# V projection in tiles of one token block by eight heads, placed behind each step's scores

## The reference

```python
x = x + 0.5 * ffn(layernorm(x))          # 256 -> 1024, gelu, -> 256
x = x + attention(layernorm(x))          # 16 heads of 64, causal, ALiBi slopes, out projection 1024 -> 256
x = x + 0.5 * ffn(layernorm(x))          # the same ffn weights
```

## Time and profile before

| | us |
|---|---|
| median of 3 runs (lowest to highest) | 2167.85 (2166.65 to 2169.6) |
| the profiled execution | 2166.86 |
| its span, first to last instruction | 2165.1 |
| mean granted TensorE clock, share of full | 0.995 |
| busy in the span: TensorE, VectorE, ScalarE, GpSimd | 2127.4, 1498.8, 1238.3, 1054.7 |

### The profile page before, as it was taken

One profiled execution on the slowest core, in us unless ns is written; L12 is line 12 of the kernel. 1 busy time (PEld: TensorE's weight loads), 2 busy tenths in 40 slices (PEclk: granted clock), 3 DMA queues, 4 the chain that ended last, 5 costly groups with the idle time before them and its releaser, 6 DMA issues.

```text
span 2165.1 us, 41849 instructions
## 1 busy us (share of the span) xinstructions
PE 2127.4 (98%) x14720; PEld 1738.5 (80%) x14720; DVE 1498.8 (69%) x4029; ACT 1238.3 (57%) x3111; POOL 1054.7 (49%) x1770
## 2 busy tenths in 40 slices
PE   7999999999999999999999999999999999999997
PEld 5688787877878788787887878878787787878876
DVE  6766767667676676776768676676766767667664
ACT  4755746466464664736557365574646646466472
POOL 1744727446273553726537174462744627355371
PEclk9999999999999999999999999999999999999999
DMA  3422505234061341514315052250523405143151
GB/s 132 130 76 71 143 3 157 59 88 128 9 159 50 108 107 35 153 29 121 95 50 142 24 141 75 72 141 3 157 59 93 123 13 155 50 111 105 35 141 41
DMA packets 109985, 193.91 MB, mean 90 GB/s; under 512 B 34512, under 2 KB 53200, under 8 KB 109776
## 3 DMA queue, kind: packets, MB, share of 16 engines
q1 hardware_dynamic: 88816, 137.95, 22.7%
q0 software_dynamic: 20480, 52.47, 9.8%
q10 hardware_dynamic: 480, 0.82, 0.1%
HBM read 14.95 MB, written 8.39 MB: 11 GB/s over the span
## 4 chain that ended last, share of the span: by engine, by line
PE 92%; DVE 3%; ACT 1%; POOL 1%; SPq 1%; DMA 1%; issue 1%; POOLq 0%; DVEq 0%; ACTq 0%
PE ps L304 90%; PE ps L358 2%; DVE P L842 1%; SPq L247 1%; POOL P L1005 1%; ACT P L641 1%; POOL PT L247 0%; DMA PT<-P 0%; DVE gl L752 0%; DVE P L834 0%; DMA raw<-in_L_ffn_w 0%; DVE gh L801 0%; DVE st L761 0%; ACT gt L610 0%; DMA out_y<-x 0%
## 5 line engine op out<-in xcount | busy, mean ns | idle before, releaser
L1005 POOL TENSOR_SCALAR P<-P,rs 128x512 f32<-128x512 f32 (+3 forms) x1024 | 539.4, 546 | 419.9 <-DVE rs L825 416.5
L641 ACT ACTIVATE P<-P,mx 128x512 f32<-128x512 f32 (+3 forms) x1024 | 562.7, 552 | 183.9 <-DVE mx L834 183.6
L247 POOL DMA_DIRECT2D PT<-P x640 | 321.8, 508 | 250.4 <-DVE P L842 231.8
L842 DVE STREAM_TRANSPOSE P<-P 128x1792 f32<-128x1792 f32 (+1 forms) x256 | 372.3, 1483 | 7.2 <-POOL P L1005 6.6
L304 PE MATMUL ps<-PT,v 128*64 128x256 f32 (+1 forms) x3072 | 308.4, 350 | 11.3 <-DMA PT<-P 11.2
L304 PE MATMUL ps<-qk 64*128 64x512 f32 (+3 forms) x2048 | 311.0, 443 | 0.7 <-ACT qk L592 0.7
L304 PE MATMUL ps<-w2h,gh 128*128 128x256 f32 x1024 | 292.8, 286 | 0.5 <-DVE gl L752 0.5
L304 PEld LDWEIGHTS ps<-PT,v 128*64 128x64 f32 x3072 | 206.4, 138 | 107.9 <-issue 18.7
L304 PE MATMUL ps<-w2l,gh 128*128 128x256 f32 x1024 | 289.7, 283 | 0.0
L304 PE MATMUL ps<-w2h,gl 128*128 128x256 f32 x1024 | 289.6, 283 | 0.0
L592 ACT ACTIVATE qk<-ps 128x512 f32<-128x512 f32 x256 | 153.0, 598 | 230.6 <-PE ps L304 230.4
(11 more groups left out here) (85 smaller groups left out, 4387.7 us busy)
## 6 DMA issues: line engine op xcount, KB each, us to landing
PT<-P SPq DMA_DIRECT2D x1398, 80.0 KB, 2.6
PT<-P POOLq DMA_DIRECT2D x640, 80.0 KB, 2.7
x<-in_L_attn_x SPq DMA_DIRECT2D x16, 512.0 KB, 4.7
out_y<-x SPq DMA_DIRECT2D x15, 512.0 KB, 3.2
raw<-in_L_ffn_w SPq DMA_DIRECT2D x2, 512.0 KB, 5.9
raw<-in_L_ffn_w SPq DMA_DIRECT2D x1, 1024.0 KB, 8.8
rawq<-in_L_attn_w_qkv SPq DMA_DIRECT2D x1, 1024.0 KB, 7.2
rawk<-in_L_attn_w_qkv SPq DMA_DIRECT2D x1, 1024.0 KB, 9.3
```

Of the source, the lines that this page charges most:

```text
L247: e.dma_start(PT[c % 2][32 * m:32 * m + 32, g, :], P[c % 3][32 * g:32 * g + 32, m, :]).then_inc(landed.sem, 16)
L641: e.activation(p, p, ACT.Exp, bias=mx[:, r, i:i + 1], scale=-1.0, accum_out=sm[:, r, i:i + 1]).then_inc(s_ex.sem, 1)
L842: e.transpose(p, p).then_inc(s_tr.sem, 1)
L1005: e.tensor_scalar(p, p, rs[:, 2 * (c % 2) + h, i:i + 1], 1.0, ALU.mult, ALU.mult).then_inc(s_nz.sem, 1)
```

## The change

A V tile becomes one token block by eight heads: six matmuls with 512 columns moving, still one PSUM bank. There are still eight tiles: three stand at the front, and one in each of the steps 2 to 6. In a step the V tile now comes straight behind the scores, ahead of k and q; ScalarE copies it ahead of k, and copies q behind exps 2. The two V buffers hold eight heads each (8 KB per partition instead of 4 KB), so one serves the pairs 0 to 3 and the other 4 to 7. The 8 KB for that come from the space reserved for the descriptors of GpSimd's DMAs, which is cut to 8192 bytes; the kernel's own buffers begin at 8320 instead of 16512.

```diff
-    at = [16512]
+    at = [8320]
...
-    v = [place(f"v{i}", [128, NT, 4, DH], F32, V + 4096 * i) for i in range(2)]
+    v = [place(f"v{i}", [128, NT, 8, DH], F32, V + 8192 * i) for i in range(2)]
...
     def v_tiles(c):
-        return {6: [("v", 3, 0), ("v", 3, 1)], 7: []}.get(c, [("v", c // 2, c % 2)] if c >= 2 else [])
+        return {2: [("v", 0, 3)], 3: [("v", 1, 0)], 4: [("v", 1, 1)], 5: [("v", 1, 2)], 6: [("v", 1, 3)]}.get(c, [])
 
-    tiles = [("k", 0), ("q", 0), ("v", 0, 0), ("v", 0, 1)]
-    FIRST = 4
+    tiles = [("k", 0), ("q", 0), ("v", 0, 0), ("v", 0, 1), ("v", 0, 2)]
+    FIRST = 5
...
                 if tile[0] == "v":
-                    _, g, u = tile
-                    gs = slice(2 * HD + g * 256, 2 * HD + g * 256 + 256)
-                    for j in range(2):
-                        ts = slice((2 * u + j) * 128, (2 * u + j) * 128 + 128)
-                        last = three(dst[:, j * 256:j * 256 + 256],
-                                     [(xth[:, k, ts], xtl[:, k, ts], wqh[:, k, gs], wql[:, k, gs])
-                                      for k in range(NK)])
+                    _, g, t = tile
+                    gs = slice(2 * HD + g * 512, 2 * HD + g * 512 + 512)
+                    ts = slice(t * 128, t * 128 + 128)
+                    last = three(dst, [(xth[:, k, ts], xtl[:, k, ts], wqh[:, k, gs], wql[:, k, gs])
+                                       for k in range(NK)])
...
-                e.wait_ge(s_pc.sem, s_pc.at((b, ("v", c // 2, 1))))
+                e.wait_ge(s_pc.sem, s_pc.at((b, ("v", c // 4, 3))))
...
                 for c in range(2, NC):
                     scores(b, c)
+                    for tile in steps_v(b, c):
+                        proj_tile(b, tile)
                     if c + 1 < NC:
                         proj_tile(b, ("k", c + 1))
                         proj_tile(b, ("q", c + 1))
-                    for tile in steps_v(b, c):
-                        proj_tile(b, tile)
...
                     exps(b, c, 3)
+                    for tile in steps_v(b, c):
+                        proj_copy(b, tile)
                     if c + 1 < NC:
                         proj_copy(b, ("k", c + 1))
+                    exps(b, c, 2)
+                    if c + 1 < NC:
                         proj_copy(b, ("q", c + 1))
-                    exps(b, c, 2)
-                    for tile in steps_v(b, c)[:1]:
-                        proj_copy(b, tile)
                     exps(b, c, 0)
-                    for tile in steps_v(b, c)[1:]:
-                        proj_copy(b, tile)
                     exps(b, c, 1)
...
-    nc = bacc.Bacc("TRN2", target_bir_lowering=False, num_devices=1)
+    nc = bacc.Bacc("TRN2", target_bir_lowering=False, num_devices=1, dynamic_dma_scratch_size=8192)
```

More of the change, by code:

```diff
@@ L63, in build @@
     R = at[0]
-    QK, V, PP, PT_AT, GT = R, R + 8192, R + 16384, R + 47104, R + 67584
+    QK, V, PP, PT_AT, GT = R, R + 8192, R + 24576, R + 55296, R + 75776
     qk = [place(f"qk{i}", [128, 2, T], F32, QK + 4096 * i) for i in range(2)]
-    v = [place(f"v{i}", [128, NT, 4, DH], F32, V + 4096 * i) for i in range(2)]
+    v = [place(f"v{i}", [128, NT, 8, DH], F32, V + 8192 * i) for i in range(2)]
     P = [place(f"P{i}", [128, 4, GW], F32, PP + 16 * GW * i) for i in range(3)]
@@ L75, in build @@
     x3h = place("x3h", [128, NK, T], F32R, QK + 4096)
-    x3l = place("x3l", [128, NK, T], F32R, V + 4096)
+    x3l = place("x3l", [128, NK, T], F32R, V + 8192)
     o_at = (PP + 10240, PT_AT + 4096, PT_AT + 12288)
@@ L111, in v_tiles @@
     def v_tiles(c):
-        return {6: [("v", 3, 0), ("v", 3, 1)], 7: []}.get(c, [("v", c // 2, c % 2)] if c >= 2 else [])
-    tiles = [("k", 0), ("q", 0), ("v", 0, 0), ("v", 0, 1)]
-    FIRST = 4
+        return {2: [("v", 0, 3)], 3: [("v", 1, 0)], 4: [("v", 1, 1)], 5: [("v", 1, 2)], 6: [("v", 1, 3)]}.get(c, [])
+    tiles = [("k", 0), ("q", 0), ("v", 0, 0), ("v", 0, 1), ("v", 0, 2)]
+    FIRST = 5
     for c in range(NC):
+        tiles += v_tiles(c)
         if c + 1 < NC:
             tiles += [("k", c + 1), ("q", c + 1)]
-        tiles += v_tiles(c)
     def steps_v(b, c):
@@ L127, in build @@
     tiles_of = {b: tiles for b in B}
-    tiles_of[0] = tiles[:8]
+    tiles_of[0] = tiles[:9]
     for c in range(1, NC):
+        tiles_of[0] = tiles_of[0] + steps_v(0, c)
         if c >= 2 and c + 1 < NC:
             tiles_of[0] = tiles_of[0] + [("k", c + 1), ("q", c + 1)]
-        tiles_of[0] = tiles_of[0] + steps_v(0, c)
     pairs = [(b, c) for b in B for c in range(NC)]
@@ L458, in values @@
                         last = mm(pv[64 * h:64 * h + 64, 128 * i:128 * i + 128 * len(blocks)],
-                                  v[(c // 2) % 2][:, j, 2 * (c % 2) + h, :], turned, n == 0, n == len(RUNS) - 1)
+                                  v[c // 4][:, j, 2 * (c % 4) + h, :], turned, n == 0, n == len(RUNS) - 1)
                 last.then_inc(s_pv.sem, 1)
@@ L468, in begin @@
                     among[0] = (6, 7)
-                    proj_tile(b, tiles[3])
+                    for tile in tiles[3:FIRST]:
+                        proj_tile(b, tile)
                 proj_tile(b, ("k", 1))
@@ L578, in proj_copy @@
                 if tile[0] == "v":
[L579 to L585, removed]
+                    _, g, r = tile
+                    if b > 0:
+                        e.wait_ge(s_pv.sem, s_pv.at((b - 1, 4 * g + 3)))
+                    dst = v[g][:, r, :, :]
+                    src = src.rearrange("p (h d) -> p h d", h=8)
                 else:
@@ L651, in attention @@
                     exps(b, 0, 3)
-                    proj_copy(b, tiles[3])
+                    for tile in tiles[3:FIRST]:
+                        proj_copy(b, tile)
                 proj_copy(b, ("k", 1))
```

## The result

| us | before | after |
|---|---|---|
| median (lowest to highest), 4 runs each | 2167.26 (2166.65 to 2169.6) | 2227.2 (2226.69 to 2227.54) |
| profiled execution, its span | 2166.86, 2165.1 | 2227.54, 2225.7 |
| mean granted TensorE clock | 0.995 | 0.983 |

The ratio is 1.0269, 95% interval 1.0257 to 1.0281: 60 us slower, 8 us more than forecast.

The account below looks back on a forecast made before the run. TensorE, busy 98% of the span, was taken as the bound. -10.0 (wider tiles) + 45.2 (bank stall) + 0.7 (DMA waits) + 1.2 (block 0) + 15.4 (clock) = +52.5 us on 2166.86, predicting 2219 us, range 2199 to 2230.

Parts of the forecast that it names:

- part 2: Step 6, blocks 1 to 14: values(b, 4) now needs the first LayerNorm unit's bank; TensorE stands 3.23 us, 45.2 us in all.
- Nothing repaid downstream: After the stall in step 6: VectorE loses its lateness at biased(b, 7), so nothing is repaid and nothing added.
- part 5: TensorE's clock falls to half speed after the new gap in 11 of 14 blocks, 1.4 us each: +15.4 us, bounds 0 to 24.
- about 3.0 are work, done at a little over half rate: Step pricing one clock fall: of some 3.3 us at low clock about 3.0 are work, so 1.4 us lost.
- the sum: All terms added to the profiled 2166.86 us; with the clock staying up, a rival at 0.25, it gives 2204 us.
- part 1: All 128 V tiles: 768 fewer matmuls at 13 ns per pair save 10.0 us, bounds 8 to 12.
- Part 3: Reordering in other steps: q copy keeps 1.3 us to spare; DMA waits +0.7 us, block 0 +1.2 us.
- No stall: the work is what counts: Rival: the bank of values(b, 4) is free before TensorE arrives, leaving mainly the wider tiles' saving: 2159 us, chance 0.06.
- The reserve: Rival: the smaller DMA reserve makes GpSimd's issues twice as long, +34 us, about 2253 us, chance 0.04.
- The change of block 0: Block 0: one more front tile ahead of k1 and q1, plus small waits, less later work: +1.2 us, bounds 0 to 3.

Follow-up runs that it names:

- e1: Changed kernel with the rotation set back after step 6's two LayerNorm units, so values(b, 4) takes q's bank: 2178.3 us, ratio 1.0051.
- e3: Kernel before, with only the bank of values(b, 4) changed to that of the first LayerNorm unit: 2216.8 us, ratio 1.0221.
- e2: Changed kernel with 11 unused 512-column matmuls issued ahead of values(b, 4) in blocks 1 to 14, filling the standstill: 2203.7 us, ratio 1.0164.
- e7: e6 with each V tile computed by twelve matmuls of 256 columns instead of six of 512: 2182.1 us, ratio 1.0061.
- e8: e1 with up(1, b+1, 6) also moved ahead of values(b, 6): 2170.3 us, ratio 1.0008.
- e6: Changed kernel with step 6's LayerNorm units moved behind values(b, 4) and up(1, b+1, 6) ahead of values(b, 6): 2175.2 us, ratio 1.0031.
- e9: e8 with the second LayerNorm unit of step 6 in bank 3 instead of bank 5: 2171.4 us, ratio 1.0014.
- e4: Kernel before, with only GpSimd's DMA reserve cut to 8192 bytes: 2169.1 us, ratio 1.0000.

## Why the prediction was right, and where it was off

**The bank (part 2): right.** The releaser, the place, the 14 blocks and the exception of block 0 came out. Without standing, values would have started at 1201.95 + 0.96 (transposes to values in the earlier trace rows) = 1202.91; they started at 1206.06: 3.15 us, forecast 3.23. The profile shows 2.6 of it as idle, because a matmul's recorded duration reaches beyond its cost. e1 removes the cause alone and gets 49 us back; e3 plants it alone in the old kernel and loses 48, clock falls included. Per block without a fall, 134.81 - 132.08 = 2.73 us were lost; my terms give 3.23 - 0.62 = 2.61.

**Nothing repaid downstream: right.** VectorE idles 2.63 us ahead of `biased(8, 7)`, and the block without a fall is longer by 2.73 us, all of the standing (3.15) less what the wider tiles save (0.49, below).

**The clock (part 5): right in kind, short in size.** This is the term that makes the 8 us. I took 11 falls of 1.4 us, 15.4 us; there were 13, and e2 prices them at 23.5 us, 1.8 each. The step that failed is "about 3.0 are work, done at a little over half rate": most falls began as the standstill ended, at block 8 with 0.50 from 1206.1 on, so that all 3.3 us of low clock were work, and values went from 2.38 to 4.04; that of block 3 was twice as long (0.50 from 523.5 to 530.1, 5.7 us of it work). In the kernel of the Trainium skill ("TensorE: Matmul & The Clock Gate", section "HAM oscillation — how this bites in real kernels") TensorE waited some 3 to 5 us for a DMA in each pass and was throttled again in each. Here a shorter wait, 2.6 us shown idle, was followed by a fall in 13 blocks of 14, and 2.1 us in e3 in 11 of 15.

Without the clock the sum was 2204 us, and e2 measured 2203.7. So close a hit is partly luck, since part 1 gave some 2 us less than its 10.

**The width (part 1): a smaller saving than 10.0 us.** The first two projection matmuls of the same step in the kernel before:

```profile
1165.14 0.50 PE L304 MATMUL ps<-xth,wqh 128*128 128x512 f32 x1
1165.48 0.40 PE L304 MATMUL ps<-xtl,wqh 128*128 128x512 f32 x1
```

In step 6 of the changed kernel V, k and q take 1201.95 - 1197.71 = 4.24 us. In the old order k, q and one V tile took 1167.99 - 1165.14 (2.85, the end by the earlier trace rows) + 1.44 = 4.29: 0.05 less in a step, not 0.08. The first matmul behind scores takes 0.33 to 0.34 to its successor in either kernel, but k, now second, takes 1.38 where a tile in the middle of a row of projections takes 1.36. With three tiles at the front at the full 0.08, that makes 0.49 us per block, about 8 us for the run, against 7 from e7; the 1.9 us by the Trainium skill's fixed cost ("TensorE: Matmul & The Clock Gate", section "Wait — 56ns, not 53.3ns?") stay well below what the starts show.

**Part 3, the other steps: right** as long as TensorE is slow enough. No new wait of weight in steps 2 to 5 (steps of 9.00 us in e1 and e8, 9.04 in the earlier trace rows). But one consequence I had not drawn: the third front tile takes 1.36 us of work out of step 6, between scores(b, 6) and values(b, 6), where ScalarE and VectorE had no room. I read the values' DMA wait in e1, the chain in e6 and e8, and the moved wait in e9 as this; no run puts the tile back to show it.

**The rivals.** "No stall: the work is what counts", 2159 us, did not happen, and e1, e6 and e8 say more: even with the stall gone the work is not what counts. **The reserve:** e4, nothing. **The change of block 0** was not measured by itself. One thing in it was not in my terms: `values(0, 0)` waits for its DMA, as before, but the clock falls behind the wait, in this and in every later kernel with three tiles at the front. First the kernel before, then the changed one:

```profile
74.39 0.87 PE L304 MATMUL ps<-PT,v 128*64 128x256 f32 x6 [2.04 <-DMA PT<-P]
74.40:78.00 3.60, 3.60 (x32) 2.48 (x34) 2.20 (x14) 3.18 (x13) 3.34 (x7) 1.00 0.86 267
...
75.89 1.69 PE L304 MATMUL ps<-PT,v 128*64 128x256 f32 x8 [2.17 <-DMA PT<-P]
76.30:79.60 3.30, 3.30 (x21) 2.40 (x19) 1.68 (x11) 3.27 (x12) 3.26 (x7) 0.50 0.94 304
```

The values take 4.00 us there instead of 2.31, start to start.

So the 60 us are 14 standstills, with 23.5 us for the clock behind them, 25.5 for the standing beyond what other waits would have taken (49 - 23.5), and 11 that stay when the bank is right (2178.3 - 2167.3; 9.5 against the runs on e1's own chip): the saving of part 1 is there, and waits for pair 6's data, for bank 5 and in block 0 eat it and more. By the starts in e1's trace, 14 blocks lose 0.72 us at pair 6's data and 0.48 at bank 5 and gain 0.49 from the wider tiles, 10 us. That is read from one block of the trace; no run separates it.

## What to carry to other kernels

Where buffers are handed out in rotation, the number of uses in a stretch is part of the schedule: adding or dropping one changes which holder the next use waits for, far from the edited lines. List for each use who held its buffer, before and after, and look up when that holder's reader runs. And before work is moved out of a stretch where the main engine seems to be the bound, ask whether the others could run that stretch any shorter.

## What the runs showed of the hardware

The granted clock fell to 0.50 after TensorE had been shown idle for 2.6 us in 13 of 14 places and not in the fourteenth (block 5), under the same instructions. With some 2.1 us idle in e3 it fell in 11 of 15 places. In block 0 it stayed up after 2.04 us and fell after 2.17. Filling the gap with matmuls whose results nobody reads made the kernel 23.5 us faster. A projection matmul of 512 columns costs 227 ns from start to start (1.36 us for six), and 0.33 to 0.34 us when it is the first behind the scores' matmuls (1165.14 to 1165.48 before, 1197.71 to 1198.04 after).
